# A decoder layer on one core: four consecutive times per partition, the context product a step ahead, row statistics from accumulated sums

## The chip, the cores and the metric

The kernel runs on one core of a Trainium2 chip. The metric is the device time of one execution in microseconds. TensorE multiplies matrices from SBUF into PSUM, VectorE, ScalarE and GpSimd work elementwise, and SyncE issues the DMAs. Each engine runs its own instructions in program order and waits for the others on semaphores that the kernel sets by hand, so the order of the code on each engine is the order on the chip.

## What is computed

Sixteen sequences x of 512 times and 512 channels go through attention, a product with a decayed context, and a quantised feed-forward layer, each with a residual and a layer norm. The change touches the first two. `_phi` is elu + 1, and the first scan decays per head.

```
qkv = x @ Wqkv.T;  q, k = _phi(q), _phi(k)
running_kv   = scan over time of k * v      # out[t] = decay * out[t-1] + in[t]
running_ksum = scan over time of k
out = q * running_kv / clip(sum_head(q * running_ksum), 1e-6)
g = sigmoid(out @ Wgate.T + bgate)
x1 = layernorm(x + (g * out + (1 - g) * v) @ Wout.T)

r[t] = 0.9 * r[t-1] + ctx[t] * ctx[t]       # context scan over time
x2 = layernorm(x1 + x1 * r)
x3 = layernorm(x2 + ffn(x2))                # ffn with 16-bit and 4-bit rounding
```

## The kernel before

`decoder` runs `prepare_weights` (to about 120 us), `attention_phase` (to 1274 us) and `ffn_phase`, one behind the other. Matrices are multiplied in float32 as two halves: a high half in fp32r, rounded by ScalarE (`xh`, `ah`, `csq_h`), and the low rest, subtracted by VectorE or GpSimd (`xl`, `al`, `csq_l`). `product` adds three matmuls a tile: high by high, low by high, high by low, each over 512 columns.

`attention_phase` has 17 steps. In step s the *front* of sequence s and the *back* of sequence s - 1 run interleaved; step 0 has only a front, step 16 only a back, and steps 2 to 15 are alike. With channels on partitions, the front makes q, k and v by tile c (`qkv`, 36 matmuls each), `phi` with two ScalarE activations and one VectorE instruction (L541), the scans of keys (L544, into `qks`) and of k * v (L553, into `kv`), and `front_product`. Then come the denominators by head (`denominators`), their reciprocals, a turn and a broadcast by TensorE, `quotient`, and the two halves of the result (`ah`, `al`). The back makes the gate products (`gate`, four of 12 matmuls, in the two `mix_ps` banks), tanh on ScalarE, `scale_difference` (L614) and `add_v`. Gate product m waits for `gated` m - 2, since it takes that bank again. Then `project` makes rows of time on partitions, in four groups j of 128 times; VectorE adds x (L662) and takes `bn_stats` (L666), five tiny instructions of `row_moments` make mean and variance, GpSimd the root (L413), and ScalarE normalises four groups (L460).

The context part lies behind the projection. GpSimd squares the context (L419), ScalarE rounds the square to `csq_h` (L482), GpSimd subtracts `csq_l` (L421), and TensorE makes the scan over time as a lower triangular product (`context_scan`): ten tiles of 128 x 128 powers of 0.9, so 30 matmuls, into four banks. VectorE multiplies the normalised rows with 1 + r (L576) and takes `bn_stats` again (L579).

On TensorE a step is `qkv` 0, the four gate products, `qkv` 1 to 3, projections 0 to 3 with denominators between the matmuls of 1 and the turn between 2 and 3, the broadcast, and the context scan. On VectorE `gate_first` puts the first scaled difference behind the key scan of tile 0 (L544); row statistics and halves of the next x alternate with the rest. On SyncE the next x tiles come first, each behind the `xl` that frees its buffer, then the context, then the store of x2 and the load of x rows.

Of the kernel before, what the change touches and what calls it, by code (L numbers as in the profile page):

```python
# [250 lines left out]
def attention_phase(nc, xT, x, ctx_in, b_gate, decay_in, wah, wal, x2_dram, amax_x2):  # L251
# [3 lines left out]
    with ExitStack() as ctx:  # L255
# [29 lines left out]
        stripf = kv[:, 0]  # L285
        bc_high = qks[0:2 * NH, 0].rearrange("p (c m) -> p c m", m=P)
        bc_low = qks[0:2 * NH, 1].rearrange("p (c m) -> p c m", m=P)
        strip_h = sb("strip_h", [P, T], F32R)
        strip_l = sb("strip_l", [P, T], F32R)
# [9 lines left out]
        stats = [sb(f"stats{n}", [P, TT, 6]) for n in range(2)]  # L299
        msum = [sb(f"msum{n}", [P, TT]) for n in range(2)]  # L300
        mdiff = [sb(f"mdiff{n}", [P, TT]) for n in range(2)]
        msq = [sb(f"msq{n}", [P, TT]) for n in range(2)]
# [12 lines left out]
        scan_banks = [mix_ps[0][:], mix_ps[1][:], qk_ps[1][:, 0], qk_ps[1][:, 1]]  # L315
# [17 lines left out]
        stats_ready = [sem("stats1_ready"), sem("stats2_ready")]  # L333
        moments_ready = [sem("moments1_ready"), sem("moments2_ready")]
        square_ready = [sem("square1_ready"), sem("square2_ready")]
# [4 lines left out]
        sq_ready, sqh_ready, sql_ready, scan_ready = sem("sq_ready"), sem("sqh_ready"), sem("sql_ready"), sem("scan_ready")  # L340
# [4 lines left out]
        with nc.Block() as block:  # L345
            @block.sync
            def _(sp):
# [4 lines left out]
                def step(s, front, back, nxt):  # L352
# [20 lines left out]
                step(0, True, False, True)  # L373
                with sp.Fori(0, (NB - 2) // 2) as i:
                    for u in range(2):
                        step(2 * i + 1 + u, True, True, True)
                step(NB - 1, True, True, False)
                step(NB, False, True, False)
# [3 lines left out]
            def _(pool):  # L382
# [4 lines left out]
                pool.memset(c09[:], XDECAY).then_inc(const_pool, 1)  # L387
# [11 lines left out]
                                   base=0, pattern=[[-1, T]], channel_multiplier=1).then_inc(const_pool, 1)  # L399
# [34 lines left out]
            def _(act):  # L434
# [27 lines left out]

                def step(s, par, front, back, nxt, due=True):
                    if front:
                        front_tile(s, 0, par)
                    if back:
                        for m in range(KC):
                            act.wait_ge(gate_ready, KC * (s - 1) + m + 1)
                            bank = mix_ps[(m + 1) % 2]
                            act.activation(bank[:], bank[:], ACT.Tanh, scale=0.5,  # L470
                                           bias=half_bg[:, m:m + 1]).then_inc(tanh_ready, 1)
                            if m == 0 and due:
                                normalise(1, s - 1)
# [5 lines left out]
                    if back:  # L479
                        act.wait_ge(sq_ready, s)  # L480
                        wait(act, scan_ready, TT * (s - 1) if not isinstance(s, int) or s > 1 else 0)
# [30 lines left out]
            def _(dve):  # L512
# [23 lines left out]
                def front_scans(b, c, par, between=None):  # L536
# [9 lines left out]
                    if between:  # L546
                        between()
# [1218 lines left out]
```

## Time and profile before

| | us |
|---|---|
| median of 3 runs (2917.76 to 2923.19) | 2918.53 |
| the profiled execution | 2919.28 |
| its span, first to last instruction | 2917.5 |
| TensorE, VectorE, ScalarE, GpSimd busy in the span | 2698, 2137, 1261, 525 |

The page gives for each engine its busy time, the granted clock of TensorE in slices, the chain that ended last and the costliest groups of instructions. Shares of the whole span mix three phases, so the views below cut out single steps of the attention phase. A timeline row has the start in us, the duration in us, the engine, the line of the code, the operation, the tiles and, in brackets, the idle time before it with what ended it. Matmuls overlap: what one costs in a row of them is the distance of their starts.

### The profile page before, as it was taken

The page shows a single profiled execution, that of the slowest core. Times are in us where ns is not written, and L with a number is a line of the kernel's source. Part 1 is how long each engine was busy: PE and PEld are TensorE (multiplying, and loading weights), DVE is VectorE, ACT ScalarE, POOL GpSimd, SP SyncE. Part 2 cuts the span into 40 slices and gives each one's busy share as a digit, 9 for nine tenths or more (in the row PEclk, how much of TensorE's full clock was granted, in tenths as well). Part 3 has the DMA queues.
Part 4 walks back from the last instruction along what each step waited for, and adds up shares of the span by engine and source line. Part 5 has one row for each costly group of instructions (what it writes and reads, how often), then busy time and mean ns, then how long its engine had stood idle before and what let it go on. Part 6 is the DMA issues. An engine that isn't in the chain of part 4 may idle for free.

```text
span 2917.5 us, 33447 instructions
## 1 busy us (share of the span) xinstructions
PE 2698.0 (92%) x12016; PEld 2217.1 (76%) x12016; DVE 2136.6 (73%) x2561; ACT 1260.9 (43%) x1426; POOL 524.9 (18%) x306
## 2 busy tenths in 40 slices
PE   2489999999999999849999999999999969999998
PEld 2477777777777777738888888788888858888886
DVE  8668888888888888844454445698787776676664
ACT  2234433334434434333333333688888842222322
POOL 4211111111111111110000000132122133234332
PEclk8689999999999999969999999999999989999999
DMA  6311111111111111144454453777777673554453
GB/s 230 123 44 58 58 58 58 58 66 70 58 58 58 58 58 58 58 166 152 159 167 171 144 165 126 270 283 266 257 260 252 243 283 124 218 232 198 187 215 123
DMA packets 146957, 429.21 MB, mean 147 GB/s; under 512 B 74848, under 2 KB 83296, under 8 KB 106592
## 3 DMA queue, kind: packets, MB, share of 16 engines
q1 hardware_dynamic: 143312, 402.43, 38.1%
q10 hardware_dynamic: 3600, 26.22, 2.2%
q8 instruction: 24, 0.39, 0.1%
q14 instruction: 21, 0.17, 0.0%
HBM read 234.62 MB, written 177.21 MB: 141 GB/s over the span
## 4 chain that ended last, share of the span: by engine, by line
PE 51%; DMA 1%; issue 1%; DVE 1%; ACT 1%; POOL 0%; SPq 0%; POOLq 0%; DVEq 0%; ACTq 0%
PE ff_ps L1665 12%; PE ff_ps L1666 12%; PE ff_ps L1667 12%; PE ff_ps L1702 5%; PE ff_ps L1704 5%; PE ff_ps L1703 5%; DMA ff_q<-x_ints 0%; DMA ff_gs<-gate_ints 0%; DMA ff_w_stage<-w_ffn_t 0%; DMA up_products<-ff_group 0%; DVE ff_wl L1381 0%; DVE ff_lo L1609 0%; ACT ff_group L1225 0%; DMA x_ints<-ff_up_abs 0%; ACT ff_group L1340 0%
## 5 line engine op out<-in xcount | busy, mean ns | idle before, releaser
L1665 PE MATMUL ff_ps<-ff_hi,ff_wh 128*128 128x512 f32 x1536 | 599.7, 390 | 42.0 <-DVE ff_lo L1387 38.8
L1667 PE MATMUL ff_ps<-ff_hi,ff_wl 128*128 128x512 f32 x1536 | 599.0, 390 | 0.0
L1666 PE MATMUL ff_ps<-ff_lo,ff_wh 128*128 128x512 f32 x1536 | 599.0, 390 | 0.0
L1225 ACT ACTIVATE ff_group<-ff_ps,ff_scales 128x512 f32<-128x512 f32 x384 | 257.8, 686 | 316.8 <-PE ff_ps L1667 306.2
L1665 PEld LDWEIGHTS ff_ps<-ff_hi,ff_wh 128*128 128x128 f32 x1536 | 289.4, 188 | 103.1 <-DVE ff_lo L1387 39.2
L1666 PEld LDWEIGHTS ff_ps<-ff_lo,ff_wh 128*128 128x128 f32 x1536 | 289.5, 188 | 60.0
L1667 PEld LDWEIGHTS ff_ps<-ff_hi,ff_wl 128*128 128x128 f32 x1536 | 289.2, 188 | 60.2
L1702 PE MATMUL ff_ps<-ff_wh,ff_hi 128*128 128x512 f32 x768 | 300.0, 391 | 24.6 <-DVE ff_lo L1603 24.0
L1703 PE MATMUL ff_ps<-ff_wl,ff_hi 128*128 128x512 f32 x768 | 299.6, 390 | 0.0
L1704 PE MATMUL ff_ps<-ff_wh,ff_lo 128*128 128x512 f32 x768 | 299.5, 390 | 0.0
L1398 DVE TENSOR_REDUCE ff_gate_max<-ff_group 128x2048 f32 (+1 forms) x48 | 109.7, 2286 | 219.7 <-ACT ff_group L1225 219.7
L1361 ACT ACTIVATE ff_hi<-ff_sr 128x2048 fp32r<-128x2048 int16 x47 | 90.2, 1919 | 338.0 <-PE ff_ps L1704 334.9
L719 PE MATMUL qk_ps<-xh,wah 128*128 128x512 f32 x512 | 201.4, 393 | 24.8 <-DVE xl L533 24.8
L1609 DVE TENSOR_TENSOR ff_lo<-ff_sr,ff_hi 128x2048 fp32r<-128x2048 int16 x47 | 109.3, 2325 | 138.2 <-ACT ff_hi L1361 138.2
L720 PE MATMUL qk_ps<-xl,wah 128*128 128x512 f32 x512 | 201.1, 393 | 0.0
L723 PE MATMUL qk_ps<-xh,wal 128*128 128x512 f32 x512 | 200.8, 392 | 0.0
L1702 PEld LDWEIGHTS ff_ps<-ff_wh,ff_hi 128*128 128x128 f32 x768 | 144.7, 188 | 55.5 <-issue 24.4
L451 ACT ACTIVATE phi<-qk_ps 128x1024 f32<-128x1024 f32 x64 | 65.9, 1029 | 262.6 <-PE qk_ps L723 262.6
L1387 DVE TENSOR_TENSOR ff_lo<-ff_q,ff_hi 128x512 fp32r<-128x512 int16 x128 | 79.9, 686 | 124.5 <-ACT ff_hi L1219 124.5
L1703 PEld LDWEIGHTS ff_ps<-ff_wl,ff_hi 128*128 128x128 f32 x768 | 144.7, 188 | 30.1
L1704 PEld LDWEIGHTS ff_ps<-ff_wh,ff_lo 128*128 128x128 f32 x768 | 144.6, 188 | 30.1
L1419 DVE CUSTOM_DVE_ANT_0 ff_up_abs<-ff_gs,ff_up_abs 128x512 f32<-128x512 int16 x192 | 156.7, 869 | 0.0
(198 smaller groups left out, 5338.4 us busy)
## 6 DMA issues: line engine op xcount, KB each, us to landing
gate_products<-ff_group SPq DMA_DIRECT2D x48, 1024.0 KB, 4.0
ff_raw<-gate_products SPq DMA_DIRECT2D x48, 1024.0 KB, 5.6
up_products<-ff_group SPq DMA_DIRECT2D x48, 1024.0 KB, 4.3
ff_raw<-up_products SPq DMA_DIRECT2D x48, 1024.0 KB, 9.3
gate_ints<-ff_gs SPq DMA_DIRECT2D x48, 512.0 KB, 2.6
ff_gs<-gate_ints SPq DMA_DIRECT2D x48, 512.0 KB, 9.9
xt_raw<-in_xT SPq DMA_DIRECT2D x64, 256.0 KB, 2.8
csq<-in_ctx_rows SPq DMA_DIRECT2D x16, 1024.0 KB, 6.1
```

The lines of the kernel that those rows point to most:

```text
L719: pe.matmul(out, sh, mh, start=(k == 0), stop=False)
L720: pe.matmul(out, sh, ml, start=False, stop=False)
L723: mm = pe.matmul(out, sl_, mh, start=False, stop=(k == n - 1))
L1225: act.activation(group[:, g, m * T:(m + 1) * T], out_ps[(GM * g + m) % 6][:], ACT.Copy, scale=s_x).then_inc(evacuated, 1)
L1398: dve.tensor_reduce(gate_max[:, 0, bass.ds(t, 1)], group[:, g], AX.X, ALU.max).then_inc(gate_max_ready, 1)
L1419: dve.tensor_tensor_reduce(up_abs[:, sl, cols], gs16[:, g, cols], up_abs[:, sl, cols], 1.0, -3e38, ALU.mult, ALU.max, cells[:, sl, m:m + 1 ...
L1665: pe.matmul(o, wh[:, m, k], hi[:, par, k], start=(k == 0), stop=False)
L1666: pe.matmul(o, wh[:, m, k], lo[:, par, k], start=False, stop=False)
L1667: mm = pe.matmul(o, wl[:, m, k], hi[:, par, k], start=False, stop=(k == KC - 1))
L1702: pe.matmul(o, hi[:, sl, k, rows], mh, start=(g == 0 and k == 0), stop=False)
L1703: pe.matmul(o, hi[:, sl, k, rows], ml, start=False, stop=False)
L1704: mm = pe.matmul(o, lo[:, sl, k, rows], mh, start=False, stop=(g == NG - 1 and k == KC - 1))
```

## The change

Time t = 4p + j of a sequence now lies on partition p in group j; before it was t = 128j + p. The host arrays x_rows and ctx_rows and the output are laid out so, and the projection takes every fourth column of `ah` and `al` as its stationary tile. With that the context scan is split: three additions along j within a partition (`local_sums`), one triangular product over partitions of the last sum (`context_carry`, three matmuls with powers of 0.9 to the fourth), and four additions of the carried part (`carried_sums`). The square moves to ScalarE, the low half to VectorE, both now for the sequence of the next step, with a second buffer `csq`.

Row statistics no longer use `bn_stats`. The additions that make the rows also give out their sum (`accum_out`), a tiny instruction makes the negative mean, and ScalarE squares the centred row with an accumulated sum (`squares`); `variance` follows. The order of the step changes on all engines: on VectorE the first scaled difference moves to the end of the step before, in front of the next phi, and the second stands behind phi 0; the second norm's squares stand between the tanh instructions on ScalarE, its normalisation behind them. SyncE issues the context load first, without a wait.

The diff, cut to its core:

```diff
-        csq = sb("csq", [P, TT, HID])
-        csq_h = sb("csq_h", [P, TT, HID], F32R)
-        csq_l = sb("csq_l", [P, TT, HID], F32R)
+        csq = sb("csq", [P, 2, TT, HID])
+        csq_h = sb("csq_h", [P, HID], F32R)
+        csq_l = sb("csq_l", [P, HID], F32R)
...
+                def step(s, par, front, back, nxt):
+                    if front:
+                        sp.dma_start(csq[:, 1 - par], ctx_in[s]).then_inc(ctx_landed, 16)
...
-                    if front:
-                        wait(sp, sql_ready, s)
-                        sp.dma_start(csq[:], ctx_in[s]).then_inc(ctx_landed, 16)
...
-                        pool.wait_ge(ctx_landed, 16 * s)
-                        pool.tensor_tensor(csq[:], csq[:], csq[:], ALU.mult).then_inc(sq_ready, 1)
-                        pool.wait_ge(sqh_ready, s)
-                        pool.tensor_tensor(csq_l[:], csq[:], csq_h[:].bitcast(F32), ALU.subtract).then_inc(sql_ready, 1)
...
+                def squares(n, s, tiles):
+
+                    for j in tiles:
+                        act.wait_ge(mean_ready[n], TT * (s - 1) + j + 1)
+                        if j > 1:
+                            act.wait_ge(squared[n], TT * (s - 1) + j - 1)
+                        act.activation(squares_out[:, j % 2], xrow[:, j], ACT.Square, bias=neg_mean[n][:, j:j + 1],
+                                       accum_out=sq_sum[n][:, j:j + 1]).then_inc(squared[n], 1)
...
+                        gate_tanh(s, 0)
+                    if due:
+                        squares(1, s - 1, (0, 1))
+                    if back:
+                        gate_tanh(s, 1)
+                    if due:
+                        squares(1, s - 1, (2, 3))
+                    if back:
+                        gate_tanh(s, 2)
+                        gate_tanh(s, 3)
+                    if due:
+                        normalise(1, s - 1)
+                    if back:
                         for m in range(KC):
                             act.wait_ge(mixed, KC * (s - 1) + m + 1)
                             act.activation(ah[:, m], att[:, m], ACT.Copy).then_inc(mh_ready, 1)
...
                         front_tile(s, 2, par)
+                        act.wait_ge(ctx_landed, 16 * (s + 1))
+                        act.activation(csq[:, 1 - par], csq[:, 1 - par], ACT.Square).then_inc(sq_ready, 1)
                         front_tile(s, 3, par)
                     if nxt:
                         split_x(s + 1, (0, 1))
+                    if back:
+                        squares(0, s, (0, 1))
+                    if front:
+                        act.wait_ge(summed, (TT - 1) * (s + 1))
+                        if back:
+                            act.wait_ge(carry_ready, s)
+                        act.activation(csq_h[:], csq[:, 1 - par, TT - 1], ACT.Copy).then_inc(sqh_ready, 1)
...
+                    if back:
+                        squares(0, s, (2, 3))
...
+                    if back:
+                        normalise(0, s)
...
+                def neg_means(n, s, tiles):
+                    for j in tiles:
+                        dve.wait_ge(y_ready[n], TT * (s - 1) + j + 1)
+                        dve.tensor_scalar(neg_mean[n][:, j:j + 1], row_sum[n][:, j:j + 1], -1.0 / HID, None,
+                                          ALU.mult).then_inc(mean_ready[n], 1)
...
+                    dve.tensor_tensor(nmr[n][:], neg_mean[n][:], rstd[n][:], ALU.mult).then_inc(nmr_ready[n], 1)
+
+                def first_residual(s, j):
+                    n = TT * (s - 1) + j + 1
+                    if j == 0:
+                        dve.wait_ge(xrow_in, 16 * s)
+                    dve.wait_ge(proj_ready, n)
+                    dve.scalar_tensor_tensor(xrow[:, j], mix_ps[(j + 1) % 2][:], 0.0, xrow[:, j], ALU.add, ALU.add,
+                                             accum_out=row_sum[0][:, j:j + 1]).then_inc(y_ready[0], 1)
...
+                def local_sums(s, sl):
+
+                    dve.wait_ge(sq_ready, s)
+                    for j in range(1, TT):
+                        dve.scalar_tensor_tensor(csq[:, sl, j], csq[:, sl, j - 1], XDECAY, csq[:, sl, j],
+                                                 ALU.mult, ALU.add).then_inc(summed, 1)
+                        dve.wait_ge(summed, (TT - 1) * (s - 1) + j)
+
+                def last_sum_low(s, sl):
+                    dve.wait_ge(sqh_ready, s)
+                    dve.tensor_tensor(csq_l[:], csq[:, sl, TT - 1], csq_h[:].bitcast(F32), ALU.subtract).then_inc(sql_ready, 1)
+
+                def carried_sums(s, sl):
+
+                    dve.wait_ge(carry_ready, s)
+                    for j in range(TT):
+                        dve.scalar_tensor_tensor(csq[:, sl, j], carry_bank, XDECAY ** (j + 1), csq[:, sl, j],
+                                                 ALU.mult, ALU.add).then_inc(scanned, 1)
+
...
+                        dve.scalar_tensor_tensor(xrow[:, j], csq[:, sl, j], 1.0, xrow[:, j], ALU.add, ALU.mult,
+                                                 accum_out=row_sum[1][:, j:j + 1]).then_inc(y_ready[1], 1)
+                    neg_means(1, s, range(TT))
...
+                    if front:
+                        front_phi(s, 0)
+                    if back:
+                        scale_difference(s, 1)
+                    if due:
+                        variance(1, s - 1)
+                    if front:
+                        front_keys(s, 0, par)
+                        front_values(s, 0)
+                    if due:
+                        norm_bias(1, s - 1)
                     if back:
+                        add_v(s, 1, par)
+                        scale_difference(s, 2)
+                        add_v(s, 2, par)
+                        scale_difference(s, 3)
+                        add_v(s, 3, par)
+                    if due:
+                        largest(s - 1)
+                    if back:
...
+                        front_scans(s, 1, par)
+                        front_product(s, 1)
+                    if back:
+                        carried_sums(s, par)
+                    if front:
+                        front_scans(s, 2, par)
+                        front_product(s, 2)
+                        front_phi(s, 3)
+                        front_keys(s, 3, par)
+                    if back:
+                        first_residual(s, 0)
+                    if front:
+                        front_values(s, 3)
+                        front_product(s, 3)
+                    if nxt:
                         split_x(s + 1, (0, 1))
+                    if front:
+                        local_sums(s + 1, 1 - par)
+                    if back:
+                        first_residual(s, 1)
+                    if front:
                         reciprocals(s)
...
+                    if back:
+                        first_residual(s, 2)
                     if nxt:
                         split_x(s + 1, (2, 3))
...
+                    if front:
+                        last_sum_low(s + 1, 1 - par)
+                    if back:
+                        first_residual(s, 3)
+                    if front:
+                        quotient(s, range(KC))
+                    if back:
+                        variance(0, s)
+                    if front:
+                        quotient_low(s)
+                    if back:
+                        norm_bias(0, s)
+                    if front:
+                        difference(s, par)
+                    if back:
+                        second_residual(s, par)
+                    if front:
+                        scale_difference(s + 1, 0)
...
-                        if j < 2:
-                            pe.wait_ge(gated, KC * (s - 1) + j + 3)
+                        if j == 0:
+                            pe.wait_ge(gated, KC * (s - 1) + 3)
+                        elif j == 1:
+                            pe.wait_ge(scanned, TT * s)
                         else:
                             pe.wait_ge(y_ready[0], TT * (s - 1) + j - 1)
-                        stat = [(ah[:, k, j * P:(j + 1) * P], al[:, k, j * P:(j + 1) * P]) for k in range(KC)]
+                        stat = [tuple(h[:, k].rearrange("p (q j) -> p j q", j=TT)[:, j] for h in (ah, al)) for k in range(KC)]
...
-                        product(scan_banks[j], stat, mov).then_inc(scan_ready, 1)
+                    pe.wait_ge(gated, KC * s)
+                    product(carry_bank, [(strip_h[:], strip_l[:])], [(csq_h[:], csq_l[:])]).then_inc(carry_ready, 1)
...
+                        qkv(s, 1)
+                    if back:
+                        context_carry(s)
+                    if front:
+                        qkv(s, 2)
+                        qkv(s, 3)
                     if back:
                         project(s, (0,))
                     if front and back:
                         project(s, (1,), lambda j: denominators(s, j))
+                        project(s, (2,))
+                        project(s, (3,), lambda k: turn_reciprocals(s) if k == 1 else None)
...
-        "x_rows": np.ascontiguousarray(a["x"].reshape(NB, TT, P, HID).transpose(0, 2, 1, 3)),
-        "ctx_rows": np.ascontiguousarray(a["ctx_1024"].reshape(NB, TT, P, HID).transpose(0, 2, 1, 3)),
+        "x_rows": np.ascontiguousarray(a["x"].reshape(NB, P, TT, HID)),
```

## Rows read from the trace of the kernel before

**Rows 1.** Windows, a steady step: PE, PEld, DVE, ACT, POOL busy, clock, DMA.

```profile
593.95:663.39 69.44, 67.41 (x311) 54.78 (x310) 61.94 (x87) 28.01 (x39) 10.75 (x4) 1.00 0.16 60
```

**Rows 2.** Timeline of TensorE in that step: start, us, instruction, idle before and releaser.

```profile
602.07 0.39 PE L719 MATMUL mix_ps<-ah,wah 128*128 128x512 f32 x1
...
609.09 0.50 PE L719 MATMUL mix_ps<-ah,wah 128*128 128x512 f32 x1 [1.42 <-DVE att L614]
...
615.62 0.39 PE L719 MATMUL qk_ps<-xh,wah 128*128 128x512 f32 x1
...
655.33 0.73 PE L786 MATMUL qk_ps<-rec_turned,head_bc 32*128 32x512 f32 x2
...
656.45 0.50 PE L719 MATMUL mix_ps<-csq_h,strip_h 128*128 128x512 f32 x1
...
663.16 0.39 PE L723 MATMUL qk_ps<-csq_h,strip_l 128*128 128x512 f32 x1
663.39 0.39 PE L719 MATMUL qk_ps<-xh,wah 128*128 128x512 f32 x1
```

**Rows 3.** Timeline of TensorE, gate of step 1: first matmul, and first behind it.

```profile
187.92 0.39 PE L719 MATMUL mix_ps<-ah,wah 128*128 128x512 f32 x1
...
198.80 0.39 PE L719 MATMUL qk_ps<-xh,wah 128*128 128x512 f32 x1
```

**Rows 4.** Timeline of VectorE in the steady step.

```profile
603.82 4.57 DVE L544 TENSOR_TENSOR_SCAN qks<-decay,phi 128x512 f32<-128x512 f32 x1
...
627.07 5.63 DVE L553 TENSOR_TENSOR_SCAN kv<-decay,kv 128x512 f32<-128x512 f32 x1
...
636.93 1.22 DVE L553 TENSOR_TENSOR_SCAN kv<-decay,kv 128x512 f32<-128x512 f32 x1
...
639.73 1.23 DVE L541 SCALAR_TENSOR_TENSOR phi<-qk_ps,phi 128x1024 f32<-128x1024 f32 x1 [0.86 <-ACT phi L453]
```

**Rows 5.** Timeline of GpSimd in the steady step.

```profile
602.73 1.01 POOL L413 TENSOR_TENSOR rstd<-var_eps,mhalf 128x4 f32<-128x4 f32 x1 [13.52 <-DVE var_eps L62]
603.70 3.60 POOL L419 TENSOR_TENSOR csq<-csq 128x2048 f32<-128x2048 f32 x1
626.46 5.17 POOL L421 TENSOR_TENSOR csq_l<-csq,csq_h 128x2048 fp32r<-128x2048 f32 x1 [19.16 <-ACT csq_h L482]
```

**Rows 6.** Groups of VectorE, 240 to 1215 us: count, busy, mean ns, idle before.

```profile
L553 DVE TENSOR_TENSOR_SCAN kv<-decay,kv 128x512 f32<-128x512 f32 x56 | 129.9, 2319 | 0.0
L544 DVE TENSOR_TENSOR_SCAN qks<-decay,phi 128x512 f32<-128x512 f32 x56 | 111.8, 1996 | 1.9
...
L666 DVE BATCH_NORM_STATS2 stats<-xrow 128x6 f32<-128x512 f32 x57 | 39.5, 693 | 1.5
```

**Rows 7.** Groups of ScalarE: steady normalisation, and table loads of the whole span.

```profile
L460 ACT ACTIVATE xrow<-xrow,nmr,rstd 128x512 f32<-128x512 f32 x113 | 83.0, 805 | 71.1 <-DVE nmr L567 71.1
...
L231 ACT ACT_TABLE_LOAD x1 | 1.3, 1283 | 0.8 <-PEq L1758 0.8
L1268 ACT ACT_TABLE_LOAD x1 | 1.3, 1283 | 0.0
```

**Rows 8.** Timeline of VectorE in the feed-forward phase, an accumulating instruction.

```profile
1994.89 0.69 DVE L1419 CUSTOM_DVE_ANT_0 ff_up_abs<-ff_gs,ff_up_abs 128x512 f32<-128x512 int16 x1
1995.50 0.08 DVE L1419 DVE_READ_ACCUMULATOR2_ANT ff_cells<- 128x1 f32 x1
```

**Rows 9.** Timeline of TensorE's denominators, and the group of their weight loads.

```profile
645.14 0.96 PE L770 MATMUL qk_ps<-head_sum,qks 128*128 128x16 f32 x8
...
L770 PEld LDWEIGHTS qk_ps<-head_sum,qks 128*128 128x128 f32 x512 | 68.4, 200 | 14.2 <-DVE qks L551 10.2
```

**Rows 10.** DMA issues: KB each, median us to landing.

```profile
csq<-in_ctx_rows SPq DMA_DIRECT2D x16, 1024.0 KB, 6.1
```

**Rows 11.** Timeline of TensorE: first matmul of step 1, first of step 16.

```profile
176.71 0.79 PE L719 MATMUL qk_ps<-xh,wah 128*128 128x512 f32 x1 [2.59 <-DVE xl L533]
...
1223.31 0.50 PE L719 MATMUL mix_ps<-ah,wah 128*128 128x512 f32 x1 [4.16 <-DVE al L603]
```

More of the change, by code:

```diff
@@ L298, in attention_phase @@
         mhalf = sb("mhalf", [P, TT])
[L299 to L302, printed above, removed]
+        squares_out = sb("squares_out", [P, 2, HID])
+        row_sum = [sb(f"row_sum{n}", [P, TT]) for n in range(2)]
+        neg_mean = [sb(f"neg_mean{n}", [P, TT]) for n in range(2)]
+        sq_sum = [sb(f"sq_sum{n}", [P, TT]) for n in range(2)]
         var_eps = [sb(f"var_eps{n}", [P, TT]) for n in range(2)]
@@ L466, in step @@
                     if back:
[L467 to L473, printed above, removed]
+                        gate_tanh(s, 0)
[11 more added lines that the diff above has]
+                    if back:
                         for m in range(KC):
@@ L478, in step @@
                         front_tile(s, 1, par)
-                    if back:
-                        act.wait_ge(sq_ready, s)
-                        wait(act, scan_ready, TT * (s - 1) if not isinstance(s, int) or s > 1 else 0)
-                        act.activation(csq_h[:], csq[:], ACT.Copy).then_inc(sqh_ready, 1)
-                    if front:
                         front_tile(s, 2, par)
+                        act.wait_ge(ctx_landed, 16 * (s + 1))
+                        act.activation(csq[:, 1 - par], csq[:, 1 - par], ACT.Square).then_inc(sq_ready, 1)
                         front_tile(s, 3, par)
@@ L508, in _ @@
                 step(NB, 0, False, True, False)
+                squares(1, NB, range(TT))
                 normalise(1, NB)
@@ L630, in step @@
                 def step(s, par, front, back, nxt, due=True):
-                    def gate_first():
-                        if due:
-                            norm_bias(1, s - 1)
-                        scale_difference(s, 0)
-                    if front and back:
-                        front_scans(s, 0, par, gate_first)
-                    elif front:
-                        front_scans(s, 0, par)
-                    else:
-                        gate_first()
+                    if front:
[9 more added lines that the diff above has]
+                        norm_bias(1, s - 1)
                     if back:
                         add_v(s, 0, par)
-                        for m in range(1, KC):
-                            scale_difference(s, m)
-                            add_v(s, m, par)
+                        add_v(s, 1, par)
[6 more added lines that the diff above has]
+                    if back:
                         for m in range(KC):
@@ L659, in step @@
-                        for j in range(TT):
-                            n = TT * (s - 1) + j + 1
-                            dve.wait_ge(proj_ready, n)
-                            dve.tensor_tensor(xrow[:, j], mix_ps[(j + 1) % 2][:], xrow[:, j], ALU.add).then_inc(y_ready[0], 1)
-                            if j == 1 and front:
-                                reciprocals(s)
-                            dve.wait_ge(y_ready[0], n)
-                            dve.bn_stats(stats[0][:, j], xrow[:, j]).then_inc(stats_ready[0], 1)
-                            if j == 1 and nxt:
-                                split_x(s + 1, (0, 1))
@@ L704, in _ @@
                 step(NB, 0, False, True, False)
+                variance(1, NB)
                 norm_bias(1, NB)
@@ L805, in step @@
                     if front:
-                        for c in range(1, KC):
-                            qkv(s, c)
+                        qkv(s, 1)
[4 more added lines that the diff above has]
+                        qkv(s, 3)
                     if back:
```

137 lines of the change are left out of this document (53 added, 84 removed).

## Prediction

> **What bounds the kernel now.** I read the windows first, to find stages, then TensorE's timeline of one step of the attention phase, then VectorE's and GpSimd's rows at the moments when TensorE stood still. The change touches the attention phase alone (123 to 1274 us of the span); the weight phase before it and the feed-forward phase behind it keep their instructions and their data sizes. One steady step takes 69.4 us, of which TensorE is busy 67.4, VectorE 61.9, ScalarE 28.0 and GpSimd 10.8 [rows 1]: TensorE sets the pace, with VectorE close behind. In TensorE's row order the step ends where the next one's first matmul starts, at 663.39, and two pieces of it matter. The context scan, 30 matmuls, takes 656.45 to 663.39, 6.94 us; its last two starts are 0.23 apart, the cost of one 512-column matmul here [rows 2]. The four gate products, 48 matmuls, take 602.07 to 615.62, 13.55 us, though 48 x 0.227 is 10.9, and the idle in front of 609.09 names VectorE's L614 [rows 2]. In step 1 the same four ran from 187.92 to 198.80, 10.88 us, without a stall [rows 3]. What differs is GpSimd: its square of the context, 603.70 for 3.60 us, stands on VectorE's key scan, which then takes 4.57 us; later its subtraction, 626.46 for 5.17 us, stands on a value scan that takes 5.63 us [rows 4, 5]. Over 14 steady steps the scans mean 2.32 and 2.00 us [rows 6], while an undisturbed one takes about 1.22 (636.93) [rows 4].
>
> **The change, part by part.** *TensorE.* With four consecutive times in a partition, the scan over times becomes three local sums, one carried product and four additions. 30 matmuls fall to 3: 6.94 - 3 x 0.227 = 6.3 us less in each of 15 steps. No stage is added on TensorE; the product sits behind qkv 1 and ends some 28 us into the step: its halves come from the step before, and the fourth scaled difference, which it also waits for, is due at 23.
>
> *GpSimd and the gate stall.* Both wide GpSimd instructions go, 8.8 us of the 10.8. VectorE gets back 56 x (2.32 - 1.22) + 56 x (2.00 - 1.22) = 105 us over 14 steps, 7.5 a step [rows 6]. The stall at the gate, 13.55 - 10.88 = 2.67 us, goes with it, if nothing else makes the products wait. So TensorE's floor is 69.44 - 6.3 - 2.67 = 60.5 us a step.
>
> *VectorE.* Eight row statistics at about 0.61 from start to start (0.69 busy [rows 6]) and ten tiny moments (about 1.3 together) go: 6.2. Eight wide instructions come (three sums, four carried additions, one low half), 8 x 0.61 plus 0.4 for the three that wait on each other: 5.3. Eight means and two variances cost 0.08 each if they overlap a neighbour, 0.35 if each waits; I take 0.2, 2.0 together. The accumulator outputs are shown only in the feed-forward phase: a read of 0.08 us follows 0.61 us behind the start of its instruction [rows 8], so 0 to 0.08 each, 8 x 0.01 taken. Sum 61.9 - 7.5 - 6.2 + 7.4 = 55.6 us, five below TensorE's floor. A forecast by adding busy times would stop here; the order decides whether the five can be used, so I walked the new order by hand with row durations.
>
> *The chain that could stop TensorE* goes from the end of the last projection to gate product 2 (durations from rows of this same step, of which not all stand here): last residual and mean 0.95, four quotients 2.4, four low halves 2.4, bias 0.1 on VectorE; four normalisations 2.9, relu 1.03, exp 1.06, copy 0.5, tanh 0.66 on ScalarE; first scale 0.69; ten handovers 0.7. Together 13.4 us. TensorE has broadcast 1.1 (655.33 to 656.45 [rows 2]), qkv 0 at 36 x 0.227 = 8.2 and two gates 5.4 ahead of it: 14.7. Margin 1.3 us. The variance of the second norm is a new wait on VectorE (four squares on ScalarE, between the tanh); behind it are queued the key scan, the add of v and the low halves for the projection. They end about 28 us into the step, TensorE wants them at 44. The wait for exp of tile 3 (0.86 idle at 639.73 [rows 4]) stays as it is and keeps its small stall. VectorE reaches it about 1.3 us early.
>
> Ahead of the turned reciprocals ScalarE now has squares 0 and 1, which wait for projection 1, then the copy of the last sum and two halves of x; they end near 57.4 us, the turn at 57.7, so the broadcast at 59 does not wait.
>
> *ScalarE* gets eight squares with two operands per partition beside the data. Nearest is the normalisation, 0.805 us [rows 7]; a plain copy of the width is 0.62, and with a read like VectorE's 0.89: 0.62 to 0.89, 0.8 taken. With one more narrow copy 28.0 becomes 35; it lies beside TensorE's work except as counted in the chain.
>
> *GpSimd's root* (1.01 us [rows 5]) stays, twice a step, but now meets two-input instructions of VectorE: low halves and the key scan. If it holds them as the wide ones did, VectorE loses up to 2 x 1.0 us; if not, 0. Margins of 1.3 hide most of it; I add 0.5 us a step for this and all small handovers.
>
> *DMA.* The context load moves to the head of SyncE's step, in front of the x loads, without a wait. It still stands behind the previous step's x2 store, the wait for the row maximum and the xrow load, which come some 5 us later than now, since the second normalisation stands behind all four tanh. Issued at about 27 us and landing in 6.1 [rows 10], it is 3 us ahead of its square, whose own slack is another 3. So nothing; if it came 5 us later the fourth exp would slip.
>
> *Strided stationary.* The projection now loads its weights with every fourth column, 16 bytes apart, 48 loads a step; no such load is in the trace. Lower bound nothing: eight contiguous loads, each with a 16-column matmul, take 0.96 us, 0.12 a pair, about half of the 0.227 slot that a projection matmul gives its load to hide in. Upper bound: four times the 0.20 that a load's own record lasts, 0.80, so 0.57 x 48 = 27 us a step [rows 9]. Less than nothing is excluded, since a hidden load gives nothing back. I take nothing, nearest to the pair, and keep the rest as a rival. The Trainium skill, SBUF — State Buffer, Door 1: The DMA port swizzle, speaks against this edit: SBUF has lines of 16 bytes, full rate needs two hits in a line, and each new line costs. No row here shows it for TensorE; it gives no price, and with a load of twice the pair the step would be 0.6 us longer and the time 2798.
>
> *Ends.* Step 1 had no stall: 6.3. Step 0: TensorE idles 2.59 us for VectorE's low half of x at 176.71 [rows 11]; the low halves now stand in front of the quotients: 2.6. Behind step 15 the scan no longer keeps TensorE (6.9), but the gate waits for VectorE anyway (4.16 idle at 1223.31 now [rows 11]) and in step 16 the copies for the projection queue behind the normalisation: between 0 and 8, I take 4.
>
> **The sum.** Steady step 60.5 + 0.5 = 61.0; 14 x (69.44 - 61.0) = 118.2; with 6.3 + 2.6 + 4.0 it is 131.1 us. The profiled execution took 2919.28 us with a span of 2917.5, 0.75 above the median of three: 2919.3 - 131.1 = 2788.
>
> **Rivals.** (A) *TensorE sets the pace*, the forecast: 60.5 to 62 us a step, 2781 to 2802, with the ends' bounds 2776 to 2806. (B) *VectorE's order becomes the bound*: means at 0.35, both roots held, the halves of a stretch not meeting their margins; 2 to 4 us a step above the floor, so 14 x 5 to 14 x 7 and 13 for the ends: 2808 to 2838. For it: five us of spare in 60, margins near 1 us; against: the waits fall at different places. (C) *The strided weights do not hide*, ending slower: at each projection matmul the slot grows to the load. 131 / 16 / 48 = 0.17, so from 0.40 us a load the gain is gone; at four times the pair, 0.48, it is 12.1 us a step in 16 steps, so 2788 + 194 = 2982. For it: every element lies 16 bytes from the last. Against: the contiguous load leaves half of the slot free [rows 9], so one of twice the price still hides. What the Trainium skill says of 16-byte lines is this mechanism without its price. (D) *Square needs its own activation table*: relu, exp, tanh, copy and identity alternate now with only two table loads, 1.28 us each, in the whole trace [rows 7], and Square is not among them. Loads around the five groups of squares of a step are ten, 12.8 us; counted where they lie on the chain of 13.4 (four, 5.1 less the margin 1.3) they give 3.8 a step, 2847; all in the way, 2960. The Trainium skill, ScalarE: Activation LUTs, Table sets: the hidden batching unit, says that functions are loaded as named sets and that cheap ones fill every set; its list there does not name Square. (E) *GpSimd was not what held the scans*, so VectorE keeps its 7.5: 55.6 + 7.5 + 4 of waits is 67 a step, 2872. Against it: step 1 and the coincidences in rows 4 and 5.
>
> **How the numbers follow.** A 0.60, B 0.24, C 0.07, D 0.04, E 0.05. The range takes A and B with the unknown costs and the lighter D: 2768 to 2850, the lower end for a tail that gains 8 and a broadcast that loses its wait. What can be told from no change is about 0.2%, 6 us. Faster: A, B, E and three quarters of D, 0.92, less a little of B's unknown, 0.91; C and the rest of D slower, 0.07; within, 0.02.
>
> **What would show it.** TensorE's step at 60.5 to 62 with the gate at 10.9 us; scans at 1.2; VectorE busy near 56 a step; GpSimd's share fallen by some 140 us. Wrong, if projection matmuls start further apart than 0.23 (C), table loads appear (D), scans stay above 2 us (E), or idle time in front of gate, denominators or next qkv names VectorE (B).

## The result and the profile after

The changed kernel takes 2796.86 us, median of 4 runs (2794.68 to 2798.62), against 2918.49 us: ratio 0.958, 95% interval 0.9563 to 0.9596. The forecast was 2788, its range 2768 to 2850. The profiled execution took 2797.14 us with a span of 2795.4, 122.1 less than the span before.

The windows of one steady step answer [rows 1] (start and end, length, busy time of PE, weight loads, VectorE, ScalarE, GpSimd, granted clock, DMA share, GB/s):

```profile
604.37:665.83 61.46, 61.46 (x285) 52.70 (x284) 53.66 (x95) 34.16 (x56) 3.23 (x2) 1.00 0.18 68
```

TensorE is busy for the whole step and nothing stops it. VectorE needs 53.66 us, so 7.8 of its time are idle, and ScalarE 34.16 instead of 28. TensorE's timeline of that step answers [rows 2, 3]:

```profile
604.37 0.50 PE L788 MATMUL qk_ps<-xh,wah 128*128 128x512 f32 x1
...
612.66 0.39 PE L788 MATMUL mix_ps<-ah,wah 128*128 128x512 f32 x1
...
623.54 0.39 PE L788 MATMUL qk_ps<-xh,wah 128*128 128x512 f32 x1
...
631.70 0.39 PE L788 MATMUL mix_ps<-csq_h,strip_h 128*128 128x512 f32 x1
...
648.71 0.40 PE L788 MATMUL mix_ps<-wah,ah 128*128 128x512 f32 x1
...
652.06 1.06 PE L841 MATMUL qk_ps<-head_sum,qks 128*128 128x16 f32 x8
652.98 0.59 PE L792 MATMUL mix_ps<-wah,al 128*128 128x512 f32 x1
653.41 0.41 PE L788 MATMUL mix_ps<-wah,ah 128*128 128x512 f32 x1
...
664.71 0.73 PE L857 MATMUL qk_ps<-rec_turned,head_bc 32*128 32x512 f32 x2
```

The gate takes 623.54 - 612.66 = 10.88 us, as in the unstalled step 1 of before. The context costs three matmuls. The projection takes 664.71 - 648.71 = 16.00 us; before it took 15.23. The groups of 300 to 1000 us (count, busy, mean ns, idle in front) answer [rows 6, 7], with the weight loads among them:

```profile
L789 PEld LDWEIGHTS qk_ps<-xl,wah 128*128 128x128 f32 x364 | 68.3, 188 | 13.7
...
L463 ACT ACTIVATE squares_out<-xrow,neg_mean 128x512 f32<-128x512 f32 x92 | 65.7, 715 | 108.3 <-DVE neg_mean L595 108.3
...
L788 PEld LDWEIGHTS mix_ps<-wah,ah 128*128 128x128 f32 x176 | 55.9, 318 | 0.4
L569 DVE TENSOR_TENSOR_SCAN qks<-decay,phi 128x512 f32<-128x512 f32 x45 | 55.1, 1225 | 1.1
L580 DVE TENSOR_TENSOR_SCAN kv<-decay,kv 128x512 f32<-128x512 f32 x45 | 54.8, 1217 | 0.0
```

The scans are back at 1.22 us, and no table load goes with the squares: the trace has two in all, as before, at 0.81 and 1713.67 us. A weight load of the projection (every fourth column) lasts 318 ns where a contiguous one lasts 188.

**Where the 122.1 us come from.** The attention phase is cut where the broadcast ends and the next matmul starts, so that before the change each scan lies in the stretch behind its step:

| stretch | forecast gain | before | after | gain |
|---|---|---|---|---|
| to the first matmul of step 1 | 2.6 | 176.71 | 172.20 | 4.5 |
| step 1 | 6.3 | 62.92 | 63.44 | -0.5 |
| the 14 steps behind it | 118.2 | 972.43 (69.46 each) | 860.38 (61.46 each) | 112.1 |
| from there to the first feed-forward matmul | 4.0 | 91.58 | 87.31 | 4.3 |
| feed-forward phase | 0 | 1613.86 | 1612.07 | 1.8 |
| sum | 131.1 | | | 122.1 |

The forecast cut otherwise, from first matmul to first matmul, with the scan at the end of its own step. By that cut step 1 went from 69.86 to 63.44 us, 6.4 less, the 14 steps gain the same 112.1, and the stretch behind them grew from 84.6 to 87.3 us, 2.7 more.

The feed-forward phase is the same program; in the twelve kernels below it took 1611.5 to 1614.4 us, so the last 1.8 are scatter.

### The profile page after: what moved, and what is told of

Read it like the earlier page. It is cut to its first block, busy times and chain, and to the rows that moved or that the text cites. A ratio compares the mean times of both kernels' runs of the same rounds, so it can differ in the third digit from the quotient of the medians.

```text
span 2795.4 us, 33065 instructions
## 1 busy us (share of the span) xinstructions
PE 2600.7 (93%) x11584; PEld 2180.7 (78%) x11584; DVE 2009.5 (72%) x2689; ACT 1359.6 (49%) x1698; POOL 398.9 (14%) x274
## 4 chain that ended last, share of the span: by engine, by line
PE 54%; DMA 1%; issue 1%; DVE 1%; ACT 1%; SPq 0%; POOL 0%; POOLq 0%; DVEq 0%; ACTq 0%
PE ff_ps L1727 12%; PE ff_ps L1728 12%; PE ff_ps L1729 12%; PE ff_ps L1764 6%; PE ff_ps L1765 6%; PE ff_ps L1766 6%; DMA ff_q<-x_ints 0%; DMA ff_gs<-gate_ints 0%; DMA ff_w_stage<-w_ffn_t 0%; DVE ff_sr L1649 0%; DMA up_products<-ff_group 0%; DVE ff_wl L1443 0%; ACT ff_group L1287 0%; DMA x_ints<-ff_up_abs 0%; ACT ff_group L1402 0%
## 5 line engine op out<-in xcount | busy, mean ns | idle before, releaser
L412 POOL TENSOR_TENSOR rstd<-var_eps,mhalf 128x4 f32<-128x4 f32 x32 | 49.6, 1551 | 983.5 <-DVE var_eps L600 983.5
L463 ACT ACTIVATE squares_out<-xrow,neg_mean 128x512 f32<-128x512 f32 x128 | 91.4, 715 | 165.5 <-DVE neg_mean L595 165.5
```

## The experiments

Steps are lengths of steady steps in the profiled execution; 69.46 before and 61.46 after are the marks.

**1. Is it the strided weight load?** a_contig takes neighbouring columns:

```
-  stat = [tuple(h[:, k].rearrange("p (q j) -> p j q", j=TT)[:, j] for h in (ah, al)) for k in range(KC)]
+  stat = [(ah[:, k, j * P:(j + 1) * P], al[:, k, j * P:(j + 1) * P]) for k in range(KC)]
```

> The changed kernel, but the projection loads its stationary operand from 128 neighbouring columns instead of every fourth; which rows stand in which partition is then not the reference's, every count and size stays. Theory S (a strided weight load costs where only a short matmul covers it): the matmul behind four denominators starts 0.31 instead of 0.43 us before the next, the others 0.227 instead of 0.235; the steady step falls from 61.46 to about 60.7 us and the time from 2797 to about 2785 us. Rival R (the projection is slower because ScalarE's squares and VectorE's accumulators read and write beside it): spacing and step stay, 61.46 us, 2797 us.

Measured: 2787.05 us, ratio to before 0.9548 (0.9533 to 0.9564), step 60.69 us. TensorE's timeline of a_contig, to be laid beside 652.06 to 653.41 above:

```profile
643.14 0.39 PE L788 MATMUL mix_ps<-wah,ah 128*128 128x512 f32 x1
...
646.49 1.06 PE L841 MATMUL qk_ps<-head_sum,qks 128*128 128x16 f32 x8
647.40 0.48 PE L792 MATMUL mix_ps<-wah,al 128*128 128x512 f32 x1
647.72 0.40 PE L788 MATMUL mix_ps<-wah,ah 128*128 128x512 f32 x1
...
658.36 0.73 PE L857 MATMUL qk_ps<-rec_turned,head_bc 32*128 32x512 f32 x2
```

The projection takes 15.22 instead of 16.00 us. The matmul behind a group of denominators holds its slot for 0.32 instead of 0.43 us, at four such places and, with 0.13 of difference, behind the turn: 0.6 of the 0.78. The other 43 loads share 0.16: a 512-column matmul covers even a strided load almost wholly. Theory S holds, R falls: the squares and accumulators beside it stayed.

a_perm keeps the result and pays for the layout on the other engines:

```
+  act.activation(ah[:, m].rearrange("p (j q) -> p q j", j=TT), att[:, m].rearrange("p (q j) -> p q j", j=TT), ACT.Copy)
+  dve.tensor_tensor(al[:, m].rearrange("p (j q) -> p j q", j=TT), att[:, m].rearrange("p (q j) -> p j q", j=TT), <ah, same>, ALU.subtract)
```

> The changed kernel with the two halves of the gated output laid out so that the projection's stationary operand is contiguous again: ScalarE writes its copy 512 bytes apart, VectorE reads both inputs of the low half rearranged (one of them 16 bytes apart) and writes it contiguous; the result is the same as the changed kernel's. By theory S TensorE gains what the contiguous form gains, step 60.7 us, 2785 us, if the rearranged accesses cost no more than the plain ones (copies 0.55 and low halves 0.61 us each). If each rearranged instruction took four times as long, ScalarE and VectorE would have 6.6 and 7.3 us more a step: VectorE's idle time is 7.8 us a step, so TensorE would wait somewhere, step 61.5 to 64, 2797 to 2830 us.

Measured: 2787.50 us (2786.11 to 2787.72), ratio 0.9546 (0.9530 to 0.9562), step 60.70 us: the best version here that keeps the result, 9.4 us below the changed kernel. The groups of a_perm show what the stride costs on VectorE and ScalarE:

```profile
L715 DVE TENSOR_TENSOR al<-att,ah 128x512 fp32r<-128x512 f32 x48 | 48.7, 1077 | 0.4
L491 ACT ACTIVATE ah<-att 128x512 fp32r<-128x512 f32 x48 | 47.5, 1143 | 0.0
```

In the changed kernel they take 687 and 619 ns. That is 1.6 and 1.8 times, not four, and it lies in idle time.

a_den_once puts the sixteen denominator matmuls (two rows each in the trace, so x32) into one group:

```
-  project(s, (1,), lambda j: denominators(s, j))
+  project(s, (1,), lambda k: [denominators(s, j) for j in range(TT)] if k == 0 else None)
```

> The changed kernel with all sixteen denominator matmuls in one group inside projection 1 instead of four groups; nothing else moves. Theory S: the step loses three of the four places where a strided load has only a short matmul to cover it, 3 x (0.43 - 0.235) = 0.6 us, step 60.9 us, 2788 us. If the cost lies in all 48 loads alike (0.008 us each in the spacing, the 0.43 being the denominators' own), the step loses at most 0.2 us: 61.3, 2794 us.

Measured: 2829.35 us, steps of 62.5 and 64.1 us. Both expectations failed. TensorE's timeline of a_den_once:

```profile
666.36 4.63 PE L841 MATMUL qk_ps<-head_sum,qks 128*128 128x16 f32 x32
670.83 0.77 PE L792 MATMUL mix_ps<-wah,al 128*128 128x512 f32 x1
671.40 0.63 PE L788 MATMUL mix_ps<-wah,ah 128*128 128x512 f32 x1
671.83 0.63 PE L789 MATMUL mix_ps<-wal,ah 128*128 128x512 f32 x1
...
675.67 0.48 PE L789 MATMUL mix_ps<-wal,ah 128*128 128x512 f32 x1
675.99 0.40 PE L792 MATMUL mix_ps<-wah,al 128*128 128x512 f32 x1
676.22 0.40 PE L788 MATMUL mix_ps<-wah,ah 128*128 128x512 f32 x1
```

The group takes 4.47 us up to the next matmul, where four groups of four take 0.92 and three times 0.81, 3.3 in all. The granted clock is 1.00 (2.4 GHz) for the first 2 us of the group and 0.50 (1.2 GHz) from 670.83 to 675.67, where matmuls start 0.43 us apart; then they are back at 0.23. Over this step it is 0.95; in the changed kernel, with four groups, it stays at 1.00. What one group would save in loads can't be read from this run.

**2. Which part carries the gain?** a_scan30 issues the carried product ten times.

> The changed kernel with its carried product issued ten times, 30 matmuls as in the scan of the kernel before instead of 3; the value stays the same. If TensorE sets the pace (A): 27 x 0.227 = 6.1 us more a step, 67.6 us, 2891 us. If VectorE's order were already the bound (B), part of it would be hidden: 62 to 66 us, 2805 to 2860 us.

Measured: 2887.68 us, step 67.57: 6.11 more for 27 matmuls, 0.226 each. Rival A holds; nothing of it is hidden. Without the shorter product the changed kernel would be slower than b_pool_off, the kernel before with GpSimd's two wide instructions gone:

```
-  pool.tensor_tensor(csq[:], csq[:], csq[:], ALU.mult)
...
-  pool.tensor_tensor(csq_l[:], csq[:], csq_h[:].bitcast(F32), ALU.subtract)
...
+  act.activation(csq[:], csq[:], ACT.Square)
```

> The kernel before with both wide GpSimd instructions gone: the square is taken on ScalarE, the low half of the squares is left out (it stays zero, so the context's scan has only its high half's value); the 30 scan matmuls, the order and the statistics stay. Theory G: scans at 1.2 us, the four gate products at 10.9 instead of 13.55 us, step 69.46 - 2.67 = 66.8 us, time about 2918 - 40 = 2878 us. Rival (VectorE's old order makes the gate wait in any case): gate 13 us or more, step 69 to 69.5, 2912 to 2918 us.

Measured: 2881.62 us, ratio 0.9873 (0.9844 to 0.9902), step 66.81, 2.65 less. TensorE's timeline of b_pool_off, first gate matmul and first behind the gate, and the groups of VectorE's scans, 300 to 1000 us:

```profile
589.24 0.39 PE L718 MATMUL mix_ps<-ah,wah 128*128 128x512 f32 x1
...
600.12 0.39 PE L718 MATMUL qk_ps<-xh,wah 128*128 128x512 f32 x1
...
L543 DVE TENSOR_TENSOR_SCAN qks<-decay,phi 128x512 f32<-128x512 f32 x41 | 50.2, 1224 | 1.4
L552 DVE TENSOR_TENSOR_SCAN kv<-decay,kv 128x512 f32<-128x512 f32 x41 | 49.9, 1216 | 0.0
```

The gate takes 10.88 us. The stall in front of it was GpSimd's, with the forecast's size of 2.67. So the parts of a steady step add up: 6.11 for the product in the new order and 2.65 for GpSimd's two instructions, less 0.77 for the strided loads, are 7.99 of the 8.00 us between 69.46 and 61.46.

b_scan4 and b_both shorten the scan in the old order:

```
-  product(scan_banks[j], stat, mov).then_inc(scan_ready, 1)
+  pe.matmul(scan_banks[j], strip_h[:, 0:P], csq_h[:, j], start=True, stop=True).then_inc(scan_ready, 1)
```

> The kernel before with 4 scan matmuls a step instead of 30 (the other 26 are left out, so the scan is not the whole one); GpSimd, order and statistics stay. If TensorE alone set the pace, 26 x 0.227 = 5.9 us go from each step: 63.6 us, about 2826 us. Rival (the scan's 6.9 us were VectorE's and ScalarE's cover between the broadcast and the gate): the stall in front of the gate grows by part of what goes, step 66 to 69 us, 2865 to 2912 us.

Measured: 2919.54 us, ratio 1.0003 (0.9992 to 1.0015), step 69.45. 26 matmuls less, and nothing gained. The timeline of b_scan4, TensorE's rows and those of VectorE that end its waits:

```profile
656.52 0.74 PE L798 MATMUL mix_ps<-csq_h,strip_h 128*128 128x512 f32 x2
...
657.59 1.28 DVE L586 TENSOR_TENSOR att<-att,qk_ps 128x512 f32<-128x512 f32 x2
...
658.33 1.10 PE L798 MATMUL qk_ps<-csq_h,strip_h 128*128 128x512 f32 x2 [1.07 <-DVE att L586]
...
661.40 1.28 DVE L533 TENSOR_TENSOR xl<-xt_raw,xh 128x512 fp32r<-128x512 f32 x2
...
662.80 0.79 PE L719 MATMUL qk_ps<-xh,wah 128*128 128x512 f32 x1 [3.37 <-DVE xl L533]
...
663.39 0.63 PE L720 MATMUL qk_ps<-xl,wah 128*128 128x512 f32 x1
```

The scan had been the cover for VectorE's quotients, which free the banks of its second half, and for the low halves of x. Without it TensorE waits 1.07 and 3.37 us, and what follows starts at 1.2 GHz (granted clock 0.50 from 662.8 to 667): query, key and value product 0 take 10.33 instead of 8.16 us. So 0.66 saved ahead of them and 1.51 at the gate, which now comes later, stand against 2.2 lost.

> The kernel before with both of these: 4 scan matmuls, no wide GpSimd instruction; the old order of VectorE and ScalarE and the statistics on VectorE stay. If the two savings add up, 69.46 - 5.9 - 2.67 = 60.9 us a step, about 2782 us, and the new order and the moved statistics are worth nothing. Rival (the old order runs out of cover): step 63 to 66 us, 2815 to 2862 us.

Measured: 2903.58 us, step 68.26. The gate is down to 10.88 us here too, but the wait for x (3.39) and the slow start are the same, so the short scan makes b_pool_off 1.45 us a step worse. The savings don't add up in the old order: its step lies above the 63 to 66 us that the rival expected.

a_xl_late undoes one place of the new order, VectorE's low halves of x tiles 2 and 3:

```
-  if nxt: split_x(s + 1, (2, 3))        # in front of last_sum_low
+  if nxt: split_x(s + 1, (2, 3))        # behind quotient(s, range(KC))
```

> The changed kernel with VectorE's low halves of x tiles 2 and 3 moved back behind the four quotients, about where the kernel before has them; nothing else. If this place is what the new order is worth, query product 0 waits for them, 3.4 us a step, and starts with the clock at 1.2 GHz as in b_scan4, 2.2 us more: step 67 us, 2875 us. If the margins elsewhere take it up: 61.5 us, 2797 us.

Measured: 2882.29 us, steps of 66.4 to 67.9. TensorE's timeline of a_xl_late, first matmul of a step:

```profile
781.47 0.79 PE L788 MATMUL qk_ps<-xh,wah 128*128 128x512 f32 x1 [3.54 <-DVE xl L555]
```

3.54 us of wait and seven or more matmuls at 1.2 GHz behind it: this one place is worth 5 to 6.5 us a step. Without it the kernel with 3 matmuls has nearly the step that the one with 30 has with it (67.3 on the mean, a_scan30 67.57).

**3. How near is VectorE?** a_margin5 adds five needless additions in front of the quotients, a_bn the eight old statistics.

> The changed kernel with five needless 128 x 512 additions on VectorE in front of the quotients of each step, about 3.3 us, on the chain from the last projection to gate product 2. With the forecast's margin of 1.3 us the step grows by 2.0 to 63.5 us (2825 us); with the margin that the changed kernel's trace shows on ScalarE (0.92 idle in front of the first tanh and about 1.05 between the first scaled difference and gate product 2) by 1.3 to 62.8 us (2815 us); if VectorE's 7.8 us of idle time could be used anywhere, not at all (2797 us).

Measured: 2823.22 us, step 63.0. The timeline of a_margin5, VectorE's rows and TensorE's gate product 2:

```profile
676.17 3.60 DVE L755 TENSOR_TENSOR spare_out<-spare 128x512 f32<-128x512 f32 x5
...
679.69 0.68 DVE L652 TENSOR_TENSOR att<-att,qk_ps 128x512 f32<-128x512 f32 x1
...
690.75 0.69 DVE L679 SCALAR_TENSOR_TENSOR att<-mix_ps,att 128x512 f32<-128x512 f32 x1 [0.94 <-ACT mix_ps L473]
...
691.50 0.50 PE L795 MATMUL mix_ps<-ah,wah 128*128 128x512 f32 x1 [0.76 <-DVE att L679]
```

The quotients come 3.52 us later and the step grows by 1.55, so the margin of this chain is 2.0 us; the forecast's walk gave 1.3. Its place was right, gate product 2. The late quotients also hold value product 0, which needs a bank that they read, by 0.5 us, a place that the walk did not have; here the longer wait at gate product 2 covers it.

> The changed kernel with the eight statistics instructions of the kernel before put back on VectorE behind the residuals, as needless work (0.61 us each from start to start, 4.9 us a step); the accumulated sums stay in use. Behind residual 3 and the second residuals lie 0.6 + 2.4 = 3.1 us of them, on VectorE's way to the first scaled difference, where the changed kernel leaves 1.96 idle and about 1.05 to gate product 2. Chain theory: step 61.5 to 62.0 us, 2797 to 2805 us. If busy times alone counted (53.7 + 4.9 = 58.6 of 61.46): no change, 61.46. If VectorE's order is close to the bound elsewhere too (rival B): 63.5 to 65 us, 2825 to 2850 us.

Measured: 2811.94 us, step 61.88, 0.42 more; VectorE is busy 58.52 of it and its first scaled difference no longer waits for the tanh. So taking the eight instructions off VectorE is worth 0.4 us a steady step, not the 4.9 that they take there; the ten tiny ones were not put back, and the squares stayed on ScalarE. The total is 7 us above the range expected: the stretch behind the last step is 5.6 us longer, 4.0 of it in the wait in front of the feed-forward phase, 50.47 instead of 46.47 us.

**4. What does GpSimd hold?** a_pool_sq gives the square back to GpSimd, a_pool_late makes it wait for the carried sums first:

```
+  pool.wait_ge(ctx_landed, 16 * (s + 1))
+  wait(pool, scanned, TT * s)             # a_pool_late alone
+  pool.tensor_tensor(csq[:, 1 - par], csq[:, 1 - par], csq[:, 1 - par], ALU.mult).then_inc(sq_ready, 1)
```

> The changed kernel with the square of the context back on GpSimd (one 128 x 2048 instruction a step, as soon as the context has landed, some 34 us into the step) instead of on ScalarE. Theory G (a wide GpSimd instruction holds VectorE's instructions beside it): a scan or carried sum beside it stretches by about 3.4 us; of that 1.45 us are covered by the idle time in front of the last phi, the rest delays the denominators: step 62.5 to 63.4 us, 2812 to 2825 us. Rival N (GpSimd was not what held the scans): scans stay at 1.22 us, step 61.46, 2797 us.

Measured: 2798.64 us, step 61.45: no loss, against theory G as it was put. GpSimd's and VectorE's timelines of a_pool_sq:

```profile
639.34 3.62 POOL L417 TENSOR_TENSOR csq<-csq 128x2048 f32<-128x2048 f32 x1 [16.35 <-DMA csq<-in_ctx_rows]
639.42 2.48 DVE L633 SCALAR_TENSOR_TENSOR csq<-mix_ps,csq 128x512 f32<-128x512 f32 x4
641.82 1.21 DVE L564 SCALAR_TENSOR_TENSOR phi<-qk_ps,phi 128x1024 f32<-128x1024 f32 x1
643.06 1.22 DVE L571 TENSOR_TENSOR_SCAN qks<-decay,phi 128x512 f32<-128x512 f32 x1
```

Beside the square stand four carried sums and a phi at their usual times (2.48 and 1.22 us in the changed kernel). Each reads one input from PSUM. The next scan starts at 643.06, when the square has ended, so this run does not test a scan.

> The changed kernel with the square of the context on GpSimd as in a_pool_sq, but started only when the carried sums are done, so that it lies beside the key scan of tile 2 (two inputs in SBUF) instead of beside carried sums and phi, which read one input in PSUM. If GpSimd holds only VectorE instructions with two SBUF inputs: that scan takes about 3.6 instead of 1.22 us, the denominators come later by 2.4 less 1.45, step 62.2 to 62.5 us, 2808 to 2812 us. If GpSimd holds nothing in this kernel: scan 1.22, step 61.46, 2797 us.

Measured: 2830.63 us, steps of 62.26 and, every third, 66.65. The same two timelines of a_pool_late, and TensorE's first denominators of a long step:

```profile
599.39 1.06 PE L844 MATMUL qk_ps<-head_sum,qks 128*128 128x16 f32 x8 [0.72 <-DVE qks L577]
...
654.51 1.21 DVE L565 SCALAR_TENSOR_TENSOR phi<-qk_ps,phi 128x1024 f32<-128x1024 f32 x1
654.66 3.60 POOL L418 TENSOR_TENSOR csq<-csq 128x2048 f32<-128x2048 f32 x1 [18.98 <-DVE csq L634]
655.75 3.59 DVE L572 TENSOR_TENSOR_SCAN qks<-decay,phi 128x512 f32<-128x512 f32 x1
```

The scan, 1.22 us by itself, takes 3.59 and ends 1.08 behind the square; 62.26 is the step expected. The long steps were not expected: in every step TensorE waits 0.72 us for the denominators' keys, and in every third the clock then falls to 1.2 GHz among the denominators (granted 0.92 over the step, 1.00 over the others).

The Trainium skill, SBUF — State Buffer, Who interferes with whom, says that VectorE meets GpSimd where both its inputs come from SBUF and GpSimd reads SBUF too, and, outside the modes in which VectorE takes both port pairs, not where it has at most one SBUF input. These two runs agree: 3.59 against 1.22 us, and 2.48 us for four carried sums as without GpSimd.

## Why the prediction was right, and where not

- **TensorE sets the pace (rival A).** Right: 61.46 us lies in its 60.5 to 62, and 27 extra matmuls cost their full 6.11 us. The term for them was 6.3.
- **Gate stall, 2.67 a step.** Right: 2.65 alone (b_pool_off), scans at 1.22. Rival E is out.
- **Floor 60.5, plus 0.5 for handovers and roots.** The step is 60.69 with contiguous loads (a_contig), so the 0.5 was 0.2. In the root's meetings with VectorE it is GpSimd that waits: the root takes 1.38 and 1.85 instead of 1.01 us [rows 5], while VectorE's four low halves beside the first keep their 2.49 and the key scan beside the second its 1.23. GpSimd's busy time fell by 126 us, not 140, mainly for that reason: its 32 roots last 49.6 instead of 32.3 us.
- **Strided stationary, taken as nothing.** This step failed: 0.77 a step. The nearest row was taken for the hidden price, one slot of 0.227 for each load. But five of the 48 loads stand behind a 16- or 128-column matmul and have no such slot; they cost 0.6 of it. The load is 1.7 times the contiguous one; the turning point of rival C, 0.40, was not reached. The Trainium skill, SBUF — State Buffer, Door 1: The DMA port swizzle, says that each access that crosses to a new line of 16 bytes pays a penalty; the loads agree, 318 against 188 ns. The prediction's side sum with a load of twice the pair came to 2798, nearer than its forecast, but by luck: it spread 0.6 us over all 48 loads.
- **Step 1, 6.3, and behind step 15, 4.0.** A counting error: one scan is counted twice. By the forecast's own cut step 1 holds, 6.4, but then the scan of step 15, from 1212.06 to 1219.0, is the end of the last of the 14 steps, and the term behind step 15 counts it again: that stretch got 2.7 us longer. By the table's cut the end holds, 4.3, and the scan is missing in step 1, which got 0.5 longer. Either way 6.7 or 6.8 us of the forecast are not there.
- **Up to step 1.** 2.6 forecast, 4.5 measured; the wait for x is gone, and the first denominators start 0.9 us earlier and run 1 us shorter, for which no experiment was made.
- **The sum.** By the table's cut, 14 x 0.77 = 10.8 lost to the loads and 6.8 to the double count; 4.3 came back from the smaller handovers, 4.0 from the ends and scatter. 131.1 - 17.6 + 8.3 = 121.8, against 122.1. The likeliest value was 9 us low. That a_contig, with the loads as the forecast took them, comes out at 2787 beside its 2788 is luck: the double count and what came back nearly cancel. Two bounds of rivals are not what their terms give, and nothing hangs on them: B's 2838 is 2836, and D's 3.8 a step give 2845 in 15 steps, not 2847.
- **Rival B.** Not reached: no wait for VectorE is left in a steady step. The margins that kept it off are small: 2.0 us by way of ScalarE (a_margin5), and 3.1 us on VectorE's own way to the first scaled difference already show (a_bn). VectorE's busy time was 53.7, forecast 55.6.
- **Rival D.** Out: the square took 0.715 us, taken 0.8, without a table load.
- **What the forecast did not say.** It priced the product by its matmuls and found room for the order by walking it, but gave the new place of x's low halves credit in step 0 alone. In the old order the shorter product is worth nothing or less (b_scan4, b_both), and in the new one the place alone is worth 5 to 6.5 us in every step (a_xl_late), about what the product gives. The longer product without that place was not run, so what the shorter one would be worth there is not shown.

## What to carry to other kernels

Matmuls that were taken away here gave time back only where what they covered was moved too; look first at what the next matmul waits for, and count the slow clock behind a new wait. Price a weight load at the places where a short matmul stands in front of it, not by the mean slot. When a helper engine slows another, see which memory the held instruction reads: another moment beside other instructions may cost nothing.

## What the runs showed of the hardware that was not expected

- The clock fell without TensorE waiting for anything: late in a run of sixteen 16-column matmuls and for 4.8 us behind it the granted clock was 1.2 GHz (a_den_once). The same matmuls in four groups, with three 512-column matmuls between them, left it at 2.4.
- The granted clock is not the same in equal steps: a wait of 0.72 us ahead of the denominators cost nothing more in two steps of three and 4.4 us in the third (a_pool_late).
- GpSimd's 3.6 us instruction made a scan with both inputs in SBUF 2.4 us longer (a_pool_late) and did not touch instructions with one input in PSUM (a_pool_sq).
- A stride of 16 bytes made a weight load 1.7 times as long, and in one of its two inputs a VectorE subtraction 1.6 times; a ScalarE copy that writes 512 bytes apart took 1.8 times.
